# Moving the small work of a software pipeline between beats and engines in a transformer block

## What is computed

```python
c_proj = silu(c) @ W_mod + b_mod          # six vectors per sequence
x_norm = ln(x) * (1 + scale_a) + shift_a
q, k, v = split(x_norm @ W_qkv + b_qkv)
x = x + gate_a * (softmax(q k^T * scale) v @ W_proj + b_proj)
q_c = ln(x) @ W_qc + b_qc
k_c, v_c = split(ln(context) @ W_kvc + b_kvc)
x = x + softmax(q_c k_c^T * scale) v_c @ W_cproj + b_cproj
x_norm2 = ln(x) * (1 + scale_m) + shift_m
x = x + gate_m * (gelu(x_norm2 @ W_mlp1 + b_mlp1) @ W_mlp2 + b_mlp2)
```

## Time and profile before

| | us |
|---|---|
| runs | 415.54, 419.03, 419.09 |
| median | 419.03 |
| the profiled execution | 420.07 |
| its span | 418.3 |
| TensorE, VectorE, ScalarE, GpSimd busy | 326.1, 270.1, 245.0, 220.8 |

### The profile page before, as it was taken

The page is one execution under the profiler, slowest core; times in us unless marked ns, Lnnn a source line. Parts: engine busy times, 40 slices in busy tenths (PEclk is TensorE's granted clock), DMA queues, the critical chain, the costliest instruction groups (busy, mean ns, idle before and its releaser), DMA issues.

```text
span 418.3 us, 15717 instructions
## 1 busy us (share of the span) xinstructions
PE 326.1 (78%) x5880; PEld 213.7 (51%) x5880; DVE 270.1 (65%) x522; ACT 245.0 (59%) x459; POOL 220.8 (53%) x493
## 2 busy tenths in 40 slices
PE   3576695878778877888778878887766777999994
PEld 2343453555555655656556556665535434445442
DVE  4753766877677898878988988889636261423301
ACT  1244362856566776767767767666462427477672
POOL 7814475867575787757877677767242310211200
PEclk9999986998998999989999999999896578999999
DMA  5135367243232423324233243233120200000101
GB/s 148 50 100 140 85 163 152 57 116 92 69 104 55 125 73 109 90 64 127 77 102 90 78 128 94 73 106 90 44 81 2 78 2 2 25 27 27 50 25 50
DMA packets 65580, 33.13 MB, mean 79 GB/s; under 512 B 8391, under 2 KB 65287, under 8 KB 65543
## 3 DMA queue, kind: packets, MB, share of 16 engines
q1 hardware_dynamic: 61991, 31.77, 27.8%
q10 hardware_dynamic: 3552, 0.86, 1.0%
HBM read 4.83 MB, written 2.10 MB: 17 GB/s over the span
## 4 chain that ended last, share of the span: by engine, by line
PE 40%; SPq 16%; DVE 14%; DMA 11%; issue 11%; ACT 3%; POOL 2%; ACTq 1%; DVEq 1%; POOLq 0%
SPq L370 12%; DMA qkc_st<-qkcp 10%; PE wide L1152 7%; PE ps_o L1113 7%; PE ps_o L1160 7%; DVE mxc L726 4%; PE wide L1091 4%; SPq L405 4%; DVE x_n L704 3%; PE wide L1102 3%; PE ps_misc L1186 2%; PE ps_misc L1309 2%; PE ps_misc L1180 2%; PE ps_misc L1289 1%; POOL qkcp L534 1%
## 5 line engine op out<-in xcount | busy, mean ns | idle before, releaser
L891 ACT ACTIVATE p_c<-wide 128x1024 f32<-128x1024 f32 x64 | 65.6, 1025 | 42.5 <-PE wide L1102 42.0
L726 DVE TENSOR_REDUCE mx<-wide 128x8 f32<-128x1024 f32 x64 | 77.4, 1209 | 15.9 <-PE wide L1091 14.6
L891 ACT ACTIVATE p_s<-wide 128x1024 f32<-128x1024 f32 x64 | 65.5, 1023 | 16.4 <-PE wide L1102 15.5
L726 DVE TENSOR_REDUCE mxc<-wide 128x8 f32<-128x616 f32 x64 | 50.9, 796 | 34.9 <-PE wide L1091 34.9
L1113 PE MATMUL ps_o<-p_c,vc_m 128*32 128x128 f32 x1024 | 45.4, 300 | 0.7 <-ACT p_c L891 0.6
L1113 PE MATMUL ps_o<-p_s,v_m 128*32 128x128 f32 x1024 | 44.2, 294 | 0.0
L1091 PE MATMUL wide<-qkc_st 62*128 62x77 bf16 x512 | 21.4, 209 | 22.3 <-DMA qkc_st<-qkcp 20.4
L1091 PE MATMUL wide<-qk_st 62*128 62x128 bf16 x512 | 26.9, 228 | 14.7 <-DVE mx L726 13.0
L1091 PEld LDWEIGHTS wide<-qk_st 62*128 62x128 bf16 x512 | 15.3, 98 | 34.6 <-DVE mx L726 26.2
L1152 PE MATMUL wide<-m_nT,w_sb 128*128 128x512 f32 x64 | 31.4, 629 | 1.6 <-DVE mxc L726 1.6
L1180 PE MATMUL ps_misc<-ident,x_n 128*128 128x128 f32 x64 | 14.3, 311 | 23.3 <-DVE x_n L704 23.2
(11 more groups left out here) (140 smaller groups left out, 760.7 us busy)
## 6 DMA issues: line engine op xcount, KB each, us to landing
qkc_st<-qkcp SPq DMA_DIRECT2D x96, 128.0 KB, 2.4
qk_st<-qkp SPq DMA_DIRECT2D x94, 128.0 KB, 2.4
out<-m_out SPq DMA_DIRECT2D x8, 256.0 KB, 2.3
xs<-x SPq DMA_DIRECT2D x3, 512.0 KB, 4.1
qk_st<-nmT SPq DMA_DIRECT2D x64, 4.0 KB
qkc_st<-nmcT SPq DMA_DIRECT2D x64, 4.0 KB
ctx_sb<-ctx SPq DMA_DIRECT2D x3, 308.0 KB
w_sb<-L_xcond_W_mlp ACTq DMA_DIRECT2D x2, 256.0 KB, 2.9
```

The costliest lines, as they stand in the source:

```text
L726: nc.vector.reduce_max(mxt[:, b].rearrange("q (x r) -> q r x", r=2)[:, r], src, AX.X, negate=True).then_inc(sems[done], 1)
L891: nc.scalar.activation(dst[u % 2][:].rearrange("k x q -> k (x q)"), ps_st[:].rearrange("k s x -> k (s x)"), ACT.Exp, scale=SCALE).then_inc ...
```

## The change

- The cross attention's weights for the query and for context keys and values are centred once: TensorE multiplies `wqc_sb` and `wkvc_sb` by `cen` (identity minus 1/128) in slot 0, ScalarE writes them (`centred`). GpSimd's four copies of these weights (L612) go.
- With them the subtraction of the mean is not needed: x1 and the context are only scaled by 1/sigma, by ScalarE (`scaled`), the residual in beat 6 and the context of back1 in beat 1. VectorE normalises only x.
- x of far and the context of here share the tiles `xc_stats`, `xc_ve` and `xc_rstd` and one power of 128x4 (`rstd_xc`), behind the cross key parts on GpSimd. Statistics are in beat 3 for x, beat 5 for the context, beat 4 for x1 (right behind the residual). x is normalised and transposed in beat 7.
- GpSimd's order is now: split of the cross query, gated weights, split of self maxima 1, high parts, split of self maxima 2, power of x1 (`rstd_x1`), low parts, split of cross maxima 1, cross key parts, joint power, split of cross maxima 2. The sync queue's program is unchanged.
- Other jobs move: on TensorE the self values and the transposes of the context from beat 3 to 2, the projection from 4 to 3, cross keys and values from 5 to 4; on ScalarE the modulated x from 1 to 0 behind the exponential, the self values from 4 to 3, the copy of the context from 4 to 3, the cross keys and values from 6 to 5; on VectorE the second residual from in front of the maximum in beat 1 to behind it in beat 0, the cross turn back in beat 7 to behind the maximum.

The core of the diff (declarations, the setup of the new tiles, and the removed halves of moved pieces are left out):

```diff
@@ -84,12 +84,11 @@
-        ("max_s0", "here", 2),
-        ("ctx_t", "back1", 0), ("v", "ahead", 1),
-        ("max_s1", "here", 0), ("proj", "back1", 2),
-        ("kv_c", "back1", 1),
-        ("max_c0", "back2", 0), ("x1_t", "back1", 2), ("x_t", "far", 2),
-        ("q_c", "back1", 0)]
+        ("max_s0", "here", 2), ("v", "ahead", 1), ("ctx_t", "back1", 0),
+        ("proj", "back1", 2),
+        ("max_s1", "here", 0), ("kv_c", "back1", 1),
+        ("max_c0", "back2", 0), ("x1_t", "back1", 2),
+        ("q_c", "back1", 0), ("x_t", "far", 2)]
...
@@ -506,16 +513,35 @@
-            def rstd(kind, p):
-                L = ln[kind]
-                hold(pool, f"{kind}_stats_set", p.n + 1)
-                nc.gpsimd.tensor_scalar(L["ve"][:], L["stats"][:, :, 2], 1.0 / C, EPS, ALU.mult,
-                                        ALU.add).then_inc(sems[f"{kind}_ve_set"], 1)
-                w(pool, f"{kind}_ve_set", p.n + 1)
+            def rstd_x1(p):
+                hold(pool, "x1_stats_set", p.n + 1)
+                nc.gpsimd.tensor_scalar(x1_ve[:], x1_stats[:, :, 2], 1.0 / C, EPS, ALU.mult,
+                                        ALU.add).then_inc(sems["x1_ve_set"], 1)
+                w(pool, "x1_ve_set", p.n + 1)
                 if not p.first():
-                    w(pool, f"{kind}_n_set", p.n)
-                nc.gpsimd.tensor_tensor(L["rstd"][:], L["ve"][:], mhalf[0:L["rows"], 0:G],
-                                        ALU.pow).then_inc(sems[f"{kind}_rstd_set"], 1)
+                    w(pool, "x1_n_set", p.n)
+                nc.gpsimd.tensor_tensor(x1_rstd[:], x1_ve[:], mhalf[:, 0:G], ALU.pow).then_inc(sems["x1_rstd_set"], 1)
+
+            def rstd_xc(far, h):
+
+                count = far.n + 1 if far else h.n + 3
+                kinds = slice(0 if far else 1, 2 if h else 1)
+                n = G * (kinds.stop - kinds.start)
+                if far:
+                    hold(pool, "x_stats_set", far.n + 1)
+                if h:
+                    hold(pool, "ctx_stats_set", h.n + 1)
+                nc.gpsimd.tensor_scalar(xc_ve[:, kinds].rearrange("t k b -> t (k b)"),
+                                        xc_stats[:, kinds].rearrange("t k b v -> t (k b) v")[:, :, 2], 1.0 / C, EPS,
+                                        ALU.mult, ALU.add).then_inc(sems["xc_ve_set"], 1)
+                w(pool, "xc_ve_set", count)
+                if far and not far.first():
+                    w(pool, "x_n_set", far.n)
+                if h and not h.first():
+                    w(pool, "ctx_n_set", h.n)
+                nc.gpsimd.tensor_tensor(xc_rstd[:, kinds].rearrange("t k b -> t (k b)"),
+                                        xc_ve[:, kinds].rearrange("t k b -> t (k b)"), mhalf[:, 0:n],
+                                        ALU.pow).then_inc(sems["xc_rstd_set"], 1)
...
@@ -577,27 +603,25 @@
-                if far:
-                    rstd("x", far)
+                if d:
+                    gated(d)
                 if h:
                     split_max(h, 0, mx, nm, "mx_set", "nmh_set", "nm_set", "mts_ps")
-                if d:
-                    gated(d)
                 if a:
                     high(a, qkx[:], [qkp[:, :, n] for n in range(3)], qkr[:], "qkx_set", "qk", "qk_in")
                 if h:
                     split_max(h, 1, mx, nm, "mx_set", "nmh_set", "nm_set", "mts_ps")
+                if d:
+                    rstd_x1(d)
                 if a:
                     low(a, [qkp[:, :, n] for n in range(3)], qkr[:], "qk")
                 if f:
                     split_max(f, 0, mxc, nmc, "mxc_set", "nmch_set", "nmc_set", "mtc_ps")
                 if d:
-                    rstd("x1", d)
-                if h:
-                    rstd("ctx", h)
-                if d:
                     parts(d, kcx[:].rearrange("c (b k) -> c b k", b=G), key_parts,
                           kcr[:].rearrange("c (b k) -> c b k", b=G), "kvc0_set", "kc", "qkc_in")
+                if far or h:
+                    rstd_xc(far, h)
...
@@ -793,15 +807,8 @@
-                    if t == 0 and h:
-                        arrived("c_in", h, {0: (0,), 1: (1,), 3: (2, 3, 4)})
-                        stats("ctx", h, ctx_sb)
-                    if t == 1 and z:
-                        residual(z, "projc_ps", "proj_c", "x2_set")
                     if t == 3 and d:
                         turn_back(d, "s", oT, "o_set", "oT_set", "proj_ps")
-                    if t == 7 and e:
-                        turn_back(e, "c", ocT, "oc_set", "ocT_set", "projc_ps")
...
@@ -818,7 +825,9 @@
-                    if t == 0 and far:
+                    if t == 0 and z:
+                        residual(z, "projc_ps", "proj_c", "x2_set")
+                    if far and t == (0 if far.first(2) else 3):
...
@@ -833,17 +842,17 @@
-                    if t == 5 and d:
                         hold(dve, "x1_set", d.n + 1)
                         stats("x1", d, xs)
-                    if t == 5 and far:
-                        normalise("x", far, x_of(far), "xt_ps")
+                    if t == 5 and h:
+                        arrived("c_in", h, {0: (0,), 1: (1,), 3: (2, 3, 4)})
+                        stats("ctx", h, ctx_sb)
+                    if t == 7 and e:
+                        turn_back(e, "c", ocT, "oc_set", "ocT_set", "projc_ps")
+                    if t == 7 and far:
+                        normalise(far)
                         if far.first():
                             tables(range(2, 6), 2)
-                    if t == 6 and d:
-                        normalise("x1", d, x_of(d), "x1t_ps")
-                    if t == 7 and h:
-                        normalise("ctx", h, ctx_of(h), "ctxt_ps")
...
@@ -941,6 +950,26 @@
+            def scaled(kind, p, src, ready, taken):
+
+                w(act, *ready)
+                if not p.first():
+                    w(act, taken, p.n)
+                for b in range(G):
+                    last = nc.scalar.activation(ln[kind]["xn"][:, b], src[:, batch(p, b)].rearrange("t o c -> t (o c)"),
+                                                ACT.Copy, scale=ln[kind]["rstd"][:, b:b + 1])
+                last.then_inc(sems[f"{kind}_n_set"], 1)
+
+            def centred():
+
+                act.wait_ge(sems["wcen_ps"], 1)
+                for n in range(2):
+                    for s_ in range(2):
+                        nc.scalar.activation(
+                            wdh[:, 2 + n, HALF * s_:HALF * (s_ + 1)].rearrange("c (d m) -> c d m", d=D),
+                            ps_o[:, n * C:(n + 1) * C].rearrange("c (m s d) -> c s d m", s=2, d=D)[:, s_], ACT.Copy)
+                nc.scalar.activation(wvc_sb[:], ps_o[:, 2 * C:3 * C], ACT.Copy).then_inc(sems["wdc_set"], 1)
+
...
@@ -994,11 +1008,13 @@
+                    if t == 6 and d:
+                        scaled("x1", d, xs, ("x1_rstd_set", d.n + 1), "x1t_ps")
+                    if t == 7 and f:
+                        empty_max(f, 0, "max_c0", "mtc_ps", nmcT, "nmcT_set", "mc_in")
                     if t == 7 and d:
                         w(act, "x1t_ps", d.n + 1)
                         nc.scalar.activation(x1T[:], ps_misc[BANK["x1_t"]][:, 0:GT], ACT.Copy).then_inc(sems["x1T_set"], 1)
-                    if t == 7 and f:
-                        empty_max(f, 0, "max_c0", "mtc_ps", nmcT, "nmcT_set", "mc_in")
...
@@ -1007,6 +1023,23 @@
+                    if t == 0 and a:
+
+                        w(act, "xt_ps", a.n + 1)
+                        if a.first():
+                            act.wait_ge(sems["mod_set"], 1)
+                        else:
+                            w(act, "v_ps", a.n)
+                            w(act, "qk_ps", a.n)
+                        for b in range(G):
+                            last = nc.scalar.activation(xmT[:, b * T:(b + 1) * T],
+                                                        ps_misc[BANK["x_t"]][:, GT + b * T:GT + (b + 1) * T], ACT.Identity,
+                                                        bias=column(mod[:, 0], a, b), scale=column(mod[:, 1], a, b))
+                        last.then_inc(sems["xmT_set"], 1)
+                    if t == 1 and d:
+                        scaled("ctx", d, ctx_sb, ("xc_rstd_set", d.n + 3), "ctxt_ps")
+                    if t == 3 and h and h.first():
+                        centred()
...
@@ -1291,13 +1328,16 @@
+                    if t == 2 and a:
+                        rows_v()
+                    if t == 2 and d:
+                        transposed("ctx_t", "ctx", d, S, "ctxt_ps")
+                    if t == 2 and h and h.first():
+                        pe.wait_ge(sems["cen_set"], 1)
+                        pe.wait_ge(sems["wc_in"], 16 * 2)
+                        mm(ps_o[:, 0:C], cen[:], wqc_sb[:], start=True, stop=True)
+                        mm(ps_o[:, C:3 * C], cen[:], wkvc_sb[:], start=True, stop=True).then_inc(sems["wcen_ps"], 1)
                     if t == 3 and d:
```

(19 more changed lines are left out.)

74 lines of the change are left out of this document (32 added, 42 removed).

## The result

The kernel after the change takes 463.44 us (461.93 to 466.68) against 418.76 for the kernel before on the same chip (415.54 to 419.09): ratio 1.108, 95% interval 1.100 to 1.116. The forecast was 441, with 429 to 452 as its range. The direction is right and the time is outside the range, 22 us above the forecast. The profiled execution has a span of 460.1 us against 418.3, at a mean granted clock of 0.870 against 0.939.

What follows compares the result with a forecast made beforehand. A loop of waits, no engine full, sets the 16.80 us slot. Late low halves add 14 x 1.7 = 23.8, slots 15 and 16 -2.6, slot 0 +0.6: +21.8 on 420.07, 441 as median; range 429 to 452.

Steps and rivals of the forecast that it cites:

- the slot of 18.5: One turn of the software pipeline, eight beats: forecast 8.2 + 10.3 = 18.5 us against 16.81, +1.7.
- P4 to P0: From TensorE issuing the first cross scores (beat 4) to the next scores of beat 0: 10.3 us forecast, 8.59 before.
- P0 to P4: From TensorE issuing beat 0's scores to beat 4's first cross scores: left at 8.2 us.
- The block, X: GpSimd's low halves queue behind the residual's power; the sync queue gets the first at P4 + 3.98, 2.9 us late.
- rivals 1 and 2: 1: block over early, slot 15.6, 400 us, chance 0.06. 2: first low half at P4 + 2.0 to 2.6, same, 0.04.
- From there to the end of the projection: From beat 7's transposed self scores, released by the maxima rows, to P0: 1.53 us plus 0.41 for x's transposes.
- rival 4: TensorE's longer wait between beats 6 and 0 lowers its clock; seven more slots at 0.91, +10, 451 us; chance 0.12.
- the summed case: The forecast as summed: slots of 18.1 to 18.9 us, 435 to 447 us; chance 0.70.
- (a): Last of the sync queue's late stacking DMAs lands at P4 + 10.29; the scores of the next beat 0 wait for it.
- keep their beats: VectorE's four self maxima, sums, division and turning back stay in their beats; P0 to P4 left at 8.2 us.
- my 1.5: ScalarE's four added scaled copies per slot: 1.5 us, between 1.2 and 1.8, at no cost in time.
- rival 3: Slots 2 to 5 and 8, longer before, absorb the new wait; nine slots pay, +13, 432 us; chance 0.08.

Runs made afterwards that it cites:

- a: Changed kernel with only GpSimd's low halves put back in front of the residual's power; 417.63 us, ratio 0.997 to before.
- f: Kernel before with only GpSimd's power of the residual moved in front of the low halves; 485.29 us, ratio 1.156.
- l_fill_few: Changed kernel in which TensorE repeats the residual's two transposes three times more in beat 6; 453.35 us, ratio 1.080 to before.
- b: Changed kernel with only ScalarE's modulated x put back into beat 1, behind the copy of the cross maxima; 461.28 us, ratio 1.102 to before.
- c: Changed kernel with GpSimd's low halves back before the residual's power and ScalarE's modulated x back in beat 1; 415.19 us, ratio 0.991 to before.
- h: Kernel c with VectorE's division of the self sums moved in front of the maximum of beat 2; 405.36 us, ratio 0.974 to before.
- m: Changed kernel with modulated x back in beat 1 and VectorE's division before beat 2's maximum, GpSimd's order left; 454.95 us, ratio 1.085 to before.
- e_fill: Changed kernel in which TensorE repeats self values in beat 6 and cross score matmuls in beat 7; 490.63 us, no ratio.

## Why the prediction was wrong, point by point

Against the slot of 18.5 in the sum stands one of 21.0: P4 to P0 is 11.6 for 10.3, P0 to P4 9.4 for 8.2.

**The block, X: right.** P4 + 4.05 against 3.98 in the sum, and the rows' landing P4 + 8.48 against 8.36. Shown by a and f. This also decides rivals 1 and 2: nothing ended the block early.

**"From there to the end of the projection it was 1.53, and now the transposes of x stand behind it, 0.41": the first step that failed.** 1.94 in the sum, 3.13 measured, +1.2 in nearly each slot. Both figures were durations at granted clock 1.00, put behind a wait that did not exist when they were taken. The clock was rival 4, and the rule named there from the Trainium skill ("TensorE: Matmul & The Clock Gate", HAM oscillation) had the right sign; I gave it 0.12 and priced it by a whole slot at 0.91, +10 us. It was not an alternative to the summed case but a part of it. l_fill_few takes it away: P4 to P0 10.5 instead of 11.6, with (a) then at P4 + 10.54 against the forecast 10.29.

**"P0 to P4 I leave at 8.2": the second step that failed.** It is 9.4, and three things share it. ScalarE's order: I gave the xmT block's move no price and did not name what is queued behind it, the cross maxima's copy and with it six or seven DMAs of the sync queue; undoing it gives 0.3 a slot before the next end stands (b). The collision of product and subtraction: 8.9 to 8.3 (c against h). The low clock at the start of the half: 0.4 to 0.5 (m). The first and the third add up on one path: the sync queue gets the cross maxima 0.7 later by the order (P0 + 2.57 to 2.67 in a, 1.88 to 1.98 in c) and 0.4 later by the clock (m against h), which makes P0 + 3.06, and P4 comes 6.3 behind that. The held product is a second path beside it, which ends P0 to P4 at 8.9 to 9.1 (c, b) when the first is short. I had read "keep their beats" from the order of VectorE's program alone; its durations depend on what GpSimd does beside it.

**The cost of ScalarE's copies: right.** One pair takes 0.69 and the other 0.68 (L959), together 1.37 of my 1.5, at no cost in time: in a, with all of them in, P4 to P0 is 8.4.

**The sum over slots.** The first P4 is in slot 2, the last in slot 15, and between them are 13 turns: 295.57 - 69.25 = 226.3 us before, 342.61 - 69.88 = 272.7 after, so +46.4, 3.6 each, where 1.7 each gave 22.1. A typical slot grew by 21.0 - 16.8 = 4.2, but those of before were on average 17.4, and that 0.6 was absorbed, as rival 3 had it. The first P4 comes 0.6 later, where the sum had 0.6 for slot 0 and 1.7 for slot 1. From the last P4 to the end it is 117.5 against 122.7, -5.2, where the sum had -2.6. Together +41.8, the difference of the spans. The missing 20 us are thus 24.3 in the 13 turns (46.4 - 22.1), less 1.7 in front of them and 2.6 behind. Why these two parts came out shorter than summed was not taken apart.

## What to carry to other kernels

An instruction moved ahead in an in-order queue costs what is queued behind it, and the rows of the kernel before gave that to about 0.1 us; but what runs behind a new wait must be priced at the clock that the wait leaves, and what runs beside a moved instruction at what that neighbour does to it. "Unchanged" is a term of the sum too: list what ends within 1 us of the present end of each part of the loop, for here each single repair uncovered the next. In a rearrangement with several orders, undo each alone: one pair of GpSimd instructions carried nearly the whole loss, and with three orders set anew (h_divide_first) the kernel was 2.6% faster than before.

## What the runs showed of the hardware that I had not expected

**Short waits are enough for the low clock.** TensorE had stood for 0.94 us before 222.61 and for 0.69 before 224.27, and was busy for 4.17 of the 5.96 us from P4; from 224.27 on the granted clock was 0.50 for 5.65 us, to P0 and beyond. In before the engine was busy for only 0.92 of the 2.53 us in front of 217.53 and kept 1.00, after 4.04 us without a gap. Busy shares of single stretches do not rank the two; what decides between them no run here settles.

**A VectorE product of two SBUF operands is held until a GpSimd cast or subtraction that started before it has ended.** s_o takes 0.42 alone. It takes 1.40 to 1.43 when GpSimd's subtraction of 1.16 started 0.01 to 0.04 before it, and then ends 0.28 or 0.29 behind the subtraction. The 0.55 of the kernel before is the same on a small scale: s_o started inside GpSimd's cast (208.34 to 208.94) and ended at 209.22, 0.28 behind it. The profile shows no wait, only a longer instruction. Where s_o started first, GpSimd was the one held: at 101.98 in before, 0.02 ahead of the subtraction, s_o kept its 0.42 and the subtraction took 1.43. A sum of the same shape with one operand in PSUM is not held, in c_both:

```profile
209.86 1.16 POOL L550 TENSOR_TENSOR qkp<-qkr,qkp 128x512 bf16<-128x512 f32 x1
```

```profile
209.89 0.41 DVE L767 TENSOR_TENSOR xs<-xs,ps_misc 128x256 f32 x1
```

The Trainium skill, "SBUF — State Buffer", Who interferes with whom, states the rule: a VectorE instruction with two SBUF inputs contends with a GpSimd instruction that reads SBUF, the shared ports are an exclusive lock, and the issue order decides who blocks. The traces agree in all these cases.

**More matmuls can cost a stand without a releaser.** It was 3.3 to 3.8 us at each of the four returns to the start of the slots' loop in e_fill (P0 at 145.92, 194.35, 242.91, 292.12), with 80 added matmuls per slot (48 scores, 32 values) and 30 packets on the instruction queue between 140 and 300 us where after has none. That the instruction queue is the cause is likely, not shown.
